# Local attention with its probabilities normalized before the value sum, and the value sum formed transposed

## The reference, cut to what the change computes

The whole model is four layers, each an attention and a feed-forward part. The change lies in the feed-forward part of layer 1, which is itself a small transformer with six layers (DEPTH), each a local attention and a gated feed-forward. Its input has 4 batches of 1024 positions of 128 features; there are 16 heads of 64 features and windows of 32 positions.

## Time and profile before

| | us |
|---|---|
| median of three runs | 11498.81 |
| lowest, highest | 11497.56, 11514.11 |
| the profiled execution, its own time | 11488.19 |
| its span in the trace | 11486.4 |
| TensorE busy | 8538.5 (74%) |
| VectorE busy | 6605.9 (58%) |
| ScalarE busy | 4270.5 (37%) |
| GpSimd busy | 3182.5 (28%) |

### The profile page before, as it was taken

The page is one execution under the profiler, slowest core; times in us unless marked ns, Lnnn a source line. Parts: engine busy times, 40 slices in busy tenths (PEclk is TensorE's granted clock), DMA queues, the critical chain, the costliest instruction groups (busy, mean ns, idle before and its releaser), DMA issues. The chain is left out here.

```text
span 11486.4 us, 282576 instructions
## 1 busy us (share of the span) xinstructions
PE 8538.5 (74%) x119632; PEld 6083.1 (53%) x119632; DVE 6605.9 (58%) x11875; ACT 4270.5 (37%) x6953; POOL 3182.5 (28%) x2445
## 2 busy tenths in 40 slices
PE   7996788888886878878878787787685655655457
PEld 3444666666664555555555555555454544544222
DVE  6652556655656757757667576676566344343443
ACT  3541333333335545645555455565221111111110
POOL 0110222222224535635355355363000211211000
PEclk9985888888888989989989899998897776766555
DMA  0000000000002212212122122121000000000000
GB/s 11 1 1 1 3 4 4 4 4 4 4 4 61 57 40 57 61 40 57 38 60 58 42 57 53 44 60 32 11 0 3 0 0 0 0 0 1 0 2 7
DMA packets 189952, 254.74 MB, mean 22 GB/s; under 512 B 58038, under 2 KB 84373, under 8 KB 187926
## 3 DMA queue, kind: packets, MB, share of 16 engines
q1 hardware_dynamic: 188822, 237.65, 7.8%
HBM read 27.80 MB, written 2.10 MB: 3 GB/s over the span
## 5 line engine op out<-in xcount | busy, mean ns | idle before, releaser
L1731 PE MATMUL wa_front<-w_wqkv,wa_xsT 128*128 128x512 f32 x2376 | 1203.4, 630 | 137.1 <-issue 106.0
L1657 POOL TENSOR_TENSOR XNT<-XNT 128x1024 f32<-128x1024 f32 x396 | 933.7, 2358 | 1139.1 <-DVE XNT L1832 1139.1
L1660 POOL TENSOR_TENSOR XNT<-XNT,wa_rnorm 128x1024 f32<-128x1024 f32 x396 | 753.3, 1902 | 160.9 <-DVE wa_rnorm L1840 160.9
L1731 PEld LDWEIGHTS wa_front<-w_wqkv,wa_xsT 128*128 128x128 f32 x2376 | 424.1, 199 | 493.0 <-issue 475.4
L1737 PE MATMUL wa_front<-consts,XNT 128*128 128x128 f32 x3168 | 473.2, 297 | 252.0 <-POOL XNT L1660 251.9
L1827 DVE TENSOR_TENSOR XNT<-wa_front,w_scaled 128x1024 f32<-128x1024 f32 x396 | 483.0, 1220 | 298.1 <-ACT wa_sq L1676 298.0
L1676 ACT ACTIVATE wa_sq<-wa_front 128x1024 f32<-128x1024 f32 x396 | 405.5, 1024 | 574.5 <-PE wa_front L1731 574.5
L1737 PEld LDWEIGHTS wa_front<-consts,XNT 128*128 128x128 f32 x3168 | 371.1, 150 | 304.5 <-POOL XNT L1660 304.2
L1832 DVE TENSOR_TENSOR XNT<-wa_front,w_scaled 128x512 f32<-128x512 f32 x792 | 495.2, 667 | 0.0
L1845 DVE TENSOR_REDUCE wa_norm<-wa_sq 128x16 f32<-128x1024 f32 x396 | 478.5, 1208 | 0.0
L2496 POOL COPY a3d_k<-a3x_qk 128x128 f32 x32 | 9.3, 289 | 1685.4 <-SPq L2493 1685.4
(11 more groups left out here) (553 smaller groups left out, 21264.3 us busy)
## 6 DMA issues: line engine op xcount, KB each, us to landing
wa_v_look<-wa_v_all SPq DMA_DIRECT2D x1188, 128.0 KB, 2.3
wa_v_look<-wa_v_all SPq DMA_DIRECT2D x792, 64.0 KB, 2.0
w_wqkv<-in_L_ffn_Wqkv_dram SPq DMA_DIRECT2D x6, 1024.0 KB
w_wo<-in_L_ffn_Wo_dram SPq DMA_DIRECT2D x6, 512.0 KB
w_wqkv<-in_L_ffn_Wqkv_dram SPq DMA_DIRECT2D x12, 256.0 KB
f2w_raw<-in_L_ffn_w_dram SPq DMA_DIRECT2D x48, 64.0 KB, 1.9
out_dram<-X SPq DMA_DIRECT2D x1, 2048.0 KB, 8.7
w_w<-in_L_ffn_W_dram SPq DMA_DIRECT2D x6, 341.0 KB
```

The lines of the kernel that those rows point to most:

```text
L1657: g.tensor_tensor(rot[:, at], rot[:, at], part[:, at], ALU.add).then_inc(s[summed], 1)
L1660: g.tensor_tensor(rot[:, at], rot[:, at], spread(rnorm[:, at, :], HDW), ALU.mult).then_inc(s[done], 1)
L1731: last = pe.matmul(front[:, first + i, :], xsT[:], wqkv[:, (2 * n + i) * 512:(2 * n + i + 1) * 512], start=True, stop=True)
```

```diff
-    xsT = st.sb("xsT", [P, P])
+    xsT = st.sb("xsT", [P, 2, P])
...
@@ ScalarE
+                a.activation(primed[:, 1:2], primed[:, 0:1], ACT.Sqrt)
+                root(K, "k_norm_in", "k_root")
...
-                square(K, "k_ps", "sq_k")
+                square(Q, "q_ps", "sq_q")
+                a.wait_ge(s["v_ps"], k + 1)
...
+                a.activation(v_all[:, w, :], two_banks(front, bank[K]), ACT.Copy).then_inc(s["v_ready"], 1)
             if attend is not None:
                 a.wait_ge(s["pT_ps"], k + 1)
...
+                a.activation(xsT[:, u, :], back[:, 1, 0:P], ACT.Copy).then_inc(s["xsT_ready"], 1)
...
+                    a.wait_ge(s["o_ps"], k + 1)
+                    a.activation(flat(oT[:]), two_banks(back, 0), ACT.Copy).then_inc(s["oT_ready"], 1)
                 root(Q, "q_norm_in", "q_root")
...
+                square(K, "k_ps", "sq_k")
@@ TensorE
-                            last = pe.matmul(back[n * WINDOW:(n + 1) * WINDOW, p, i * HDW:(i + 1) * HDW],
-                                             pT[r, i, n * WINDOW:(n + 1) * WINDOW],
-                                             v_look[r, w, n, i * HDW:(i + 1) * HDW], start=True, stop=True)
+                            at = i % 4 * P + n * WINDOW
+                            last = pe.matmul(back[p * HDW:(p + 1) * HDW, i // 4, at:at + WINDOW],
+                                             v_look[r, w, n, i * HDW:(i + 1) * HDW],
+                                             pT[r, i, n * WINDOW:(n + 1) * WINDOW], start=True, stop=True)
...
-                pe.wait_ge(s["o_ready"], k + 1)
-                for i in range(INNER // P):
-                    last = pe.transpose(back[:, i // 4, (i % 4) * P:(i % 4 + 1) * P],
-                                        o[:, 2 * i:2 * i + 2, :].rearrange("p h d -> p (h d)"), c.ident)
...
+                pe.wait_ge(s["xsT_ready"], k + 1)
+                if project is not None:
+                    pe.wait_ge(s["kT_ready"], k + 1)
+                product(K, bank[K], "k_ps", u)
@@ VectorE
+                v.tensor_tensor(pc[:], pc[:], spread(rtotal[:], LOOK), ALU.mult).then_inc(s["normed"], 1)
...
-                v.tensor_tensor(by_parity(o[:]), back[:].rearrange("p k (a d) -> p k a d", d=HDW),
-                                rtotal[:].rearrange("p (a k) -> p k a", k=2).unsqueeze(3).broadcast_to([P, 2, A, HDW]),
-                                ALU.mult).then_inc(s["o_ready"], 1)
```

More of the change, by code:

```diff
@@ L1742, in _ @@
                 if k >= 1:
[L1743 to L1756 removed]
                     pe.wait_ge(s["qT_ready"], k)
[L1758 removed]
+                product(Q, bank[Q], "q_ps", w)
             if score is not None:
```

122 lines of the change are left out of this document (61 added, 61 removed).

## The result

The changed kernel takes **12541.89 us** (median of four runs, 12517.37 to 12548.55), the kernel before on the same chip 11498.18 (four runs, 11490.48 to 11514.11). The ratio is **1.0902, with a 95% interval of 1.0883 to 1.0921**: slower, as forecast, but by 1044 us and not by 595. The profiled execution's span is 12546.1 us, against 11486.4, 1060 us more.

What follows compares the result with a forecast made beforehand. A loop of waits through GpSimd, no full engine, bounded the 17.60 us step. Loop 2.6 plus clock 0.5 gave 3.1 us a step, times 192 is 595 us on 11488.2: 12083 us, range 11700 to 12470.

Steps and rivals of the forecast that it cites:

- The place and the sign: Local-attention stage: slower, chance 0.90, with TensorE idle 2.6 us before the K product until the kT copy.
- The sums: Weighted sums on TensorE: 64 loads per array part, 58 ns apart, 3.9 us a step instead of 1.49.
- The rivals with 2.3 and 0.8 us: Weighted sums: closer loads, 2.3 us, 11776 us total, chance 0.11; or pace by moved columns, 0.8 us, chance 0.06.
- The bank: Weighted sums: both row halves write one PSUM bank yet overlap, taking 3.9 us, despite the skill's rule.
- The rival of 7.6 us: Weighted sums: the two halves take turns at their common bank, 7.6 us, 12794 us total, chance 0.08.
- The new loop: Attention step: TensorE and ScalarE wait for each other twice, 20.2 us at full clock instead of 17.60.
- ScalarE's chain: Between sums and next K product: hand-over, oT copy, root of Q, table load, priming, kT copy, 3.66 us together.
- The multiplication of pc: VectorE, between sums and pc transposes: 1.21 us, no delay counted from GpSimd's add, at most 2.4 us a step.
- The clock: TensorE's granted clock: more slow pieces from the longer wait before the K product, 0.5 us a step.
- two slow pieces: Attention step: two stretches at lower clock in every step, 2.5 us more a step, used for the upper end, 12470.
- The share lost before the change: Attention steps of the kernel before: 8% of the time at half speed, 1.5 us a step, losing 0.75.
- The range: Whole kernel: 11700 to 12470 us for 8 in 10, from closer loads up to 2.5 us a step of clock loss.

Runs made afterwards that it cites:

- early root: Changed kernel with ScalarE's root of Q, table load and primed exponential moved ahead of the oT copy: 12317 us.
- the order of before: Kernel before the change with only the operands of the weighted sums swapped as in the changed kernel (attention values differ): 11598 us.
- the old sums in the new order: Changed kernel with the weighted sums put back to their form before the change (attention values differ): 11945 us.
- work in the wait: Changed kernel with a second, useless Q product on TensorE behind K's transposes, before the K product: 12242 us.
- the last kernel: Against the kernel before: K product one step ahead, root early, pc transposes and xsT copy moved forward; sums and o multiplication as before: 11133.83 us, ratio 0.9713.
- sums of 256 instructions: Changed kernel with each matmul of the sums split in two, 32 weight columns each, on four array parts: 12608 us.
- the old sums with the early root: Changed kernel with the sums' form from before and ScalarE's root, table load and priming ahead of the oT copy (values differ): 11622 us.

## Why the prediction was right, and where it was not

- **The place and the sign.** Right. All of the loss is in the attention stage, and TensorE waits 2.71 us before the K product, released by the kT copy of line 1718, where 2.6 was forecast.
- **The sums.** Right: most often 3.92 us at full clock (median 4.06), for 3.9, and 4.14 in the step shown. Doubling the moving columns changed nothing, so the spacing of 58 ns by 64 weight columns was the right neighbour. The rivals with 2.3 and 0.8 us fall.
- **The bank.** Right to trust the row. The Trainium skill, "TensorEngine Tiling (Array Packing)", section "Restrictions and Gotchas", excludes different row tiles from one PSUM bank at the same time; the runs do not bear that out as a price, 3.92 us with a common bank and 3.92 with separate ones. The rival of 7.6 us falls with it.
- **The new loop.** Right within 0.3 us. In the step whose timeline is shown, from the output product of the step before (which starts at 5857.27) to the sums 10.1 us were 9.9 in the forecast, ScalarE's chain 3.70 was 3.66, from the K product to the output product 2.66 was 2.74. Steps of 20.45 instead of 20.2, 48 us over all. The early root took out the 1.5 us that the sum says it should.
- **The multiplication of pc.** Right to count nothing: 1.23 us, and GpSimd's add was over before it.
- **The clock.** Wrong, and this is the step that failed, under "The clock": I took 0.5 us a step, with 2.5 as two slow pieces at most; it was 2.43. That is 192 x 1.93 = 371 of the 461 us by which the loss in the stage exceeds the forecast; the loop brings 48 and the ends of the six passes some 40. Two things were wrong in it. I let slow pieces come from the wait alone and stretch one product, whereas the lower clock lasts 13.7 us in a row and stretches the sums to 6.9 us, on the loop itself. And I saw that the sums were thin (25344 instructions with half the moving columns) and costed only their time, not what they do to the clock beside a wait. The share lost before the change, 0.75 us a step from 600 us at 0.96, was not what failed: inside the blocks it is 0.49, and of the 1.38 us over all intervals 1.0 lies in the 48 beside the ends of blocks.
- **The range.** The time lies 72 us above it. Its upper end, 12470, was two slow pieces a step, 2.5 us; the clock took 2.43. With the 48 us of the loop and the 40 at the ends that end would have been some 12555, where the profiled execution took 12548. That the bound comes so close is luck: it was priced as pieces of 1.64 us that stretch a product, not as 7.4 us at the lower clock that stretch the sums.

What the runs show of the clock's cause: neither the thin sums alone (0.94 in the order of before, 1.00 inside the blocks) nor the wait alone decides (the steps without a stop of the old sums in the new order have 1.2 us at the lower clock, as against 1.1 before the change), and to shorten the wait from 2.71 to 1.21 us beside the thin sums gives nothing (0.81). The two together take it, and either more columns through the sums (0.92) or work in the wait (0.88) gives part of it back. This fits a clock that follows what TensorE streams over sums and waits together, but the early root, which leaves out 1.5 us of waiting and gains no clock, shows that this is no full account; what exactly decides stays open. So does whether sums in this form would pay in an order with no waits beside them, which was not tried.

## What to carry over

Cost a matmul loop with small tiles by its loads and their weight columns, not by what moves (here with 32 and 64 moving columns); where the two operands can change places, look first at what that does to the weight columns and to the number of parts of the array in use. When a change makes TensorE stream less and wait more in the same stretch, cost the clock from the slow steps of the whole stage, and put on the path every product that a slow piece may hit. A wait that can't be taken away is the place for work from elsewhere: here the o transposes, which the change had removed, stand in it in the last kernel, and the K product behind them waits for nothing more. Before a clock is put down to an order, part the steps by what happened in them: with and without a stop, inside a block and beside its end.

## What the runs showed of the hardware

- Work of no use made a kernel faster: 788 matmul instructions more in the stage, 314 us less of it, because the granted clock of the stage rose from 0.81 to 0.88.
- 64 moving columns cost no more than 32 when the weights have 64 columns (sums most often 3.95 and 3.92 us at full clock), and the wider kernel was 316 us faster through the clock (0.92 instead of 0.81).
- Two halves of the array's rows write one PSUM bank side by side as fast as two banks: 128 instructions in 3.92 us either way.
- Dense runs of tiny matmuls can stop for 2.1 to 2.2 us with no semaphore behind it: 265 times in sums of 256 instructions, 74 in sums of 128. Each time a 16 KB packet of the instruction queue lands in the stop, and the matmuls go on 1.2 to 1.6 us later.
- The lower clock goes with such a stop: in the old sums with the early root, steps with one had 6.2 us at the lower clock, steps without one 0.3.
- Thin matmuls in place of waits raised the clock: with the order of before and the new sums all 144 intervals inside the blocks ran at full clock, 59 in the kernel before.
- A VectorE operation on 128x16 numbers in SBUF took 0.17 us alone and 1.02 beside GpSimd's add.
